# Two mixture stages of a four-block vision network: gate order and Pool adds in the first, up banks and takes in the last

## What is computed

```python
def _L0_ffn_ref(x, gate_w, gate_b, W1, b1, W2, b2):        # 2048 tokens of 64, E = 8 experts of width 128
    probs = softmax(xf @ gate_w + gate_b)
    top2_vals, top2_idx = top_k(probs, 2)
    cw = zeros((N, E)).at[arange(N)[:, None], top2_idx].add(top2_vals)
    for e in range(E):
        acc = acc + cw[:, e, None] * (gelu(xf @ W1[e] + b1[e]) @ W2[e] + b2[e])

def _L3_ffn_ref(h, gate_w, gate_b, w1, b1, w2, b2):        # 8 experts of width 256
    probs = softmax(x @ gate_w + gate_b)
    idx, prb = argmax(probs), max(probs)
    pos = place of the token among those of its expert;  kept = pos < C
    y = (relu(x @ w1[idx] + b1[idx]) @ w2[idx] + b2[idx]) * (prb * kept)
    y = nan_to_num(y, nan=0.0, posinf=1e4, neginf=-1e4)
```

## Time and profile before

| what | value |
|---|---|
| three runs | 539.71, 541.76, 542.22 us (median 541.76) |
| the profiled execution's own time | 541.19 us |
| its span, first to last instruction | 539.4 us |
| mean granted clock of TensorE | 0.973 of full speed |
| PE busy | 478.7 us (89%), 5459 matmul instructions |
| DVE busy | 328.7 us (61%) |
| ACT busy | 293.0 us (54%) |
| POOL busy | 140.1 us (26%) |
| first mixture, from its first up to its last add | 126.94 to 168.71 us of the span |
| last mixture, from its first up to its last add | 464.3 to 535.9 us |

### The profile page before, as it was taken

One profiled execution on the slowest core, in us unless ns is written; L12 is line 12 of the kernel. 1 busy time (PEld: TensorE's weight loads), 2 busy tenths in 40 slices (PEclk: granted clock), 3 DMA queues, 4 the chain that ended last, 5 costly groups with the idle time before them and its releaser, 6 DMA issues. The chain is left out here.

```text
span 539.4 us, 12786 instructions
## 1 busy us (share of the span) xinstructions
PE 478.7 (89%) x5459; PEld 255.5 (47%) x5464; DVE 328.7 (61%) x575; ACT 293.0 (54%) x430; POOL 140.1 (26%) x134
## 2 busy tenths in 40 slices
PE   4799998998996999878998999997997998999992
PEld 1343432554333496778788744343223335533330
DVE  1285999455356366677777746758554593554565
ACT  2583223526651236988788636674683171665561
POOL 8170000000064000599999920003402000000000
PEclk9999999998998899999999998999899889999998
DMA  7000000002661002855565200011003000001000
GB/s 271 2 2 2 1 2 1 1 12 104 162 155 34 2 1 63 293 206 194 202 201 196 81 6 18 0 67 48 0 1 125 0 2 1 2 21 40 1 18 22
DMA packets 9801, 34.52 MB, mean 64 GB/s; under 512 B 1248, under 2 KB 2704, under 8 KB 9360
## 3 DMA queue, kind: packets, MB, share of 16 engines
q1 hardware_dynamic: 9744, 33.70, 19.5%
HBM read 32.94 MB, written 0.75 MB: 62 GB/s over the span
## 5 line engine op out<-in xcount | busy, mean ns | idle before, releaser
L1096 PE MATMUL PS<-GX,OH 128*128 128x64 f16 x1152 | 70.4, 193 | 10.0 <-DVE OH L1279 7.1
L1202 ACT ACTIVATE OHU<-BC,wbuf 128x2048 fp8e4<-128x2048 f16 x36 | 70.0, 1994 | 12.5 <-PE PS L1096 8.8
L1096 PEld LDWEIGHTS PS<-GX,OH 128*128 128x128 f16 x1152 | 67.6, 98 | 15.1 <-DVE OH L1279 8.9
L1096 PE MATMUL PS<-GX,OHU 128*128 128x64 f16 x1152 | 70.1, 193 | 0.1
L1096 PEld LDWEIGHTS PS<-GX,OHU 128*128 128x128 fp8e4 x1152 | 67.6, 98 | 0.1
L1035 POOL TENSOR_TENSOR VAL<-V 128x256 f32<-128x256 f32 x35 | 38.8, 1108 | 2.7
L708 DVE SCALAR_TENSOR_TENSOR D<-QKVP,wbuf,D 128x1024 f32<-128x1024 f32 x27 | 34.6, 1281 | 7.7 <-ACT D L608 6.9
L1032 POOL TENSOR_TENSOR V<-SQ 128x512 f32<-128x512 f32 x18 | 25.1, 1394 | 49.9 <-DVE SQ L1289 48.6
L437 PE MATMUL PS<-T,DG 128*32 128x512 f32 x336 | 37.1, 594 | 0.0
L1996 PE MATMUL PS<-Y,wbuf 64*128 64x512 f32 x128 | 35.6, 618 | 0.1
L2069 ACT ACTIVATE HID<-PS,wbuf 128x512 f32<-128x512 f32 x44 | 28.7, 689 | 10.4 <-PE PS L1996 10.3
(11 more groups left out here) (296 smaller groups left out, 920.3 us busy)
## 6 DMA issues: line engine op xcount, KB each, us to landing
BC<-idx_dram SPq DMA_DIRECT2D x36, 512.0 KB, 4.3
GB<-gate_dram SPq DMA_DIRECT2D x16, 256.0 KB, 7.2
wbuf<-pack_dram SPq DMA_DIRECT2D x1, 1913.0 KB, 9.3
wbuf<-pack_dram SPq DMA_DIRECT2D x1, 1624.0 KB, 6.7
wbuf<-pack_dram SPq DMA_DIRECT2D x1, 1494.0 KB, 6.1
wbuf<-pack_dram SPq DMA_DIRECT2D x1, 871.0 KB, 4.3
wbuf<-pack_dram SPq DMA_DIRECT2D x1, 788.0 KB, 10.8
wbuf<-pack_dram SPq DMA_DIRECT2D x1, 607.0 KB, 3.8
```

The lines of the kernel that those rows point to most:

```text
L1096: mm = pe.matmul(o, (OH, OHU)[qh][:, s % NOH, t * P:(t + 1) * P], src, start=(qh == 0 and part == 0), stop=(qh == 1 and part == 1))
L1202: act.activation(OHU[:, s % NOH, :], BC[:, s % NBC, :], ACT.Abs_reciprocal_sqrt, bias=wt("hitq"), scale=HIT, saturate=False).then_inc(uppe ...
```

## The change

In the first mixture:

- TensorE waits for the logits to be read ahead of its first up. The first seven up matmuls use seven banks (4 to 7, then 0 to 2) without a wait; later ones use banks 4 to 7. Five up steps come first, then the gates' transpose, then down 0; behind that two downs and two ups take turns to the end. Downs 0 to 2 wait until the up in their bank is emptied.
- SP loads the gates of expert 0 in two half rows (18 loads instead of 16).
- ACC is gone. VectorE adds T of expert 0 into X, GpSimd adds T of experts 1 to 6 into X, and VectorE adds T of expert 7 behind GpSimd's sum.

In the last mixture:

- From unit 24 (SIX) on, ups use six banks (6, 7, 4, 5, 2, 3); downs use two banks (0, 1) instead of three.
- In chunks of two j, the evacuation and the take of the second j are done a chunk later (`settled`). Masks have four buffers and are made at the start of a chunk's work on VectorE (`mine`).
- VectorE takes every odd hidden unit from 12 on, six more than before.
- The last j (DIRECT) is not evacuated: VectorE scales the sum so far, then reads the out bank, adds the bias, multiplies by SCB and copies by mask (`take_direct`).

```diff
@@ first mixture: SP, GpSimd, TensorE
-                for e in range(E):
-                    if e >= 4:
-                        sp.wait_ge(gates_in[e % 4], 32)
+                for j, (e, first, last) in enumerate(ROWS):
+                    if j >= 4:
+                        sp.wait_ge(gates_in[j % 4], 32 * (j // 4))
...
-                        pool.tensor_tensor(ACC[:, c], a, T[:, k % TBUF, :], ALU.add).then_inc(summed, 1)
+                        pool.tensor_tensor(X[:, c], X[:, c], T[:, k % TBUF, :], ALU.add).then_inc(summed, 1)
...
-                        if n >= 4:
-                            pe.wait_ge(hid_in, n - 3)
+                        if n >= WIDE:
+                            pe.wait_ge(hid_in, up_after(n))
...
-                    if k == 0:
-                        pe.wait_ge(g_exp, 1)
+                    if k < 3:
+                        pe.wait_ge(hid_in, 5 + k)
...
-                for k in range(4):
+                pe.wait_ge(g_exp, 1)
+                for k in range(5):
                     up(k)
-                down(0)
                 pe.wait_ge(gated, 1)
                 pe.transpose(bank(3, P), EXPS[:, :, :].rearrange("p t e -> p (t e)"), wt("ident")).then_inc(gt_ps, 1)
+                down(0)
                 down(1)
-                up(4)
                 up(5)
+                up(6)
                 down(2)
-                up(6)
+                down(3)
                 up(7)
-                down(3)
-                for first, ups in ((4, (8, 9, 10)), (6, (11, 12, 13)), (8, (14, 15))):
-                    for k in ups:
-                        up(k)
-                    down(first)
-                    down(first + 1)
-                for k in range(10, NK):
+                up(8)
+                for k in range(4, NK):
                     down(k)
+                    if k % 2 and k + 4 < NK:
+                        up(k + 4)
+                        if k + 5 < NK:
+                            up(k + 5)
@@ first mixture: VectorE
+                    if e == 0:
+                        dve.wait_ge(weighed, k + 1)
+                        dve.tensor_tensor(X[:, c], X[:, c], T[:, k % TBUF, :], ALU.add).then_inc(first_in, 1)
+                    if e == E - 1:
+                        dve.wait_ge(weighed, k + 1)
+                        dve.wait_ge(summed, pool_sum(E - 2, bp))
+                        ins = dve.tensor_tensor(X[:, c], X[:, c], T[:, k % TBUF, :], ALU.add)
@@ last mixture
-            UBANK, OBANK = (4, 5, 2, 3), (0, 1, 6)
+            OBANK = (0, 1)
+            def up_bank(n):
+                return bank((4, 5, 2, 3)[n % 4] if n < SIX else (6, 7, 4, 5, 2, 3)[(n - SIX) % 6])
+            DIRECT = NJ - 1
+            SIX = 24
+            def settled(i):
+                late = [j for j in CHUNKS[i - 1][1:] if j < DIRECT] if i else []
+                return late + [j for j in CHUNKS[i] if j == CHUNKS[i][0] or j >= DIRECT]
             def on_dve(n):
-                return n % 2 == 1 and n >= ALONE and (n < 16 or n % 8 != 7)
+                return n % 2 == 1 and n >= ALONE
...
-                        if n >= 4:
+                        if n == SIX:
+                            pe.wait_ge(cum_in, 1)
+                            pe.wait_ge(sc_row, 1)
+                        elif n > SIX:
+                            wait_hidden(pe, n + bh - 6)
+                        elif n >= 4:
                             wait_hidden(pe, n + bh - 4)
...
-                    if n % 4 == 0 and j >= 3:
-                        pe.wait_ge(out_in, j - 2)
+                    if n % 4 == 0 and j >= 2:
+                        pe.wait_ge(out_in, j - 1)
...
+                def take_direct(j):
+                    bp, e = j // E, j % E
+                    dve.wait_ge(hid_used, 4 * j + 4)
+                    after(dve, dve.scalar_tensor_tensor(out=OUT8[:, j % 2, :], in0=bank(OBANK[j % 2]), scalar=wt("b2c", e, 1),
+                                                        in1=SCB[:, bp * HC:(bp + 1) * HC], op0=ALU.add, op1=ALU.mult))
+                    after(dve, dve.copy_predicated(SUM8[:, bp, :], MINE[:, j % 4, :], OUT8[:, j % 2, :]))
...
                 for i, chunk in enumerate(CHUNKS):
+                    if len(chunk) > 1:
+                        for j in settled(i):
+                            mine(j)
                     if i + 1 < len(CHUNKS):
                         for j in CHUNKS[i + 1]:
                             for n in range(4 * j, 4 * j + 4):
                                 if on_dve(n):
                                     hidden(n)
-                    for j in chunk:
+                    for j in settled(i):
+                        if j >= DIRECT:
+                            if j == DIRECT:
+                                scaled(1)
+                            take_direct(j)
+                            continue
                         if j >= E:
                             first_half(j)
```

More of the change, by code:

```diff
@@ L787, in build, with up_after @@
             T = sb("T2", [P, TBUF, HC], F32, sctx)
[L788 to L790 removed]
+            gated, gt_ps, gt_in, gt_out, hid_ps, hid_in, hid_used, weighed, first_in, summed = (
+                sem("s2_" + n) for n in ("gated", "gt_ps", "gt_in", "gt_out", "hid_ps", "hid_in", "hid_used", "weighed", "first_in", "summed"))
             gates_in = [sem(f"s2_gates_in{i}") for i in range(4)]
             NK = 2 * E
[L793 removed]
+            WIDE = 7
+            ROWS = [(0, 0, HC), (0, HC, COLS)] + [(e, 0, COLS) for e in range(1, E)]
+            def up_bank(n):
+                return (4, 5, 6, 7, 0, 1, 2)[n] if n < WIDE else 4 + (n - WIDE) % 4
+            def up_after(n):
+                return n - 6 if n < WIDE + 4 else n - 3
             def pool_sum(e, bp):
[L797 removed]
+                return 2 * (e - 1) + bp + 1
             @block.sync
@@ L892, in _ @@
                         act.wait_ge(hid_used, n - HBUF + 1)
-                    act.activation(HID[:, n % HBUF, :], bank(4 + n % 4), ACT.Gelu, bias=wt("b1_0", n // 4, 1)).then_inc(hid_in, 1)
+                    act.activation(HID[:, n % HBUF, :], bank(up_bank(n)), ACT.Gelu, bias=wt("b1_0", n // 4, 1)).then_inc(hid_in, 1)
                 warm(act, ACT.Sqrt)
@@ L932, in _ @@
                     c = slice(bp * HC, (bp + 1) * HC)
-                    dve.wait_ge(gates_in[e % 4], 32 * (e // 4 + 1))
+                    j = bp if e == 0 else e + 1
+                    dve.wait_ge(gates_in[j % 4], 32 * (j // 4 + 1))
                     dve.wait_ge(hid_used, 2 * k + 2)
                     before = e - TBUF // 2
-                    if before in ON_POOL:
+                    if before >= 1:
                         dve.wait_ge(summed, pool_sum(before, bp))
[L938 to L951, removed]
+                    if before == 0:
+                        dve.wait_ge(first_in, bp + 1)
+                    dve.scalar_tensor_tensor(out=T[:, k % TBUF, :], in0=bank(k % 4), scalar=wt("b2_0", e, 1), in1=GB[:, e, c],
+                                             op0=ALU.add, op1=ALU.mult).then_inc(weighed, 1)
+                    if e == 0:
[5 more added lines that the diff above has]
+                        ins = dve.tensor_tensor(X[:, c], X[:, c], T[:, k % TBUF, :], ALU.add)
+                        if bp == 0:
+                            ins.then_inc(x_half, 1)
         with ExitStack() as sctx, nc.Block() as block:
@@ L2058, in evacuate @@
                     act.wait_ge(hid_used, 4 * j + 4)
-                    if e and takes(j) > 2:
-                        act.wait_ge(taken, takes(j) - 2)
+                    if e and takes(j - 2) > 0:
+                        act.wait_ge(taken, takes(j - 2))
                     o = OUT8[:, j % 2, :] if e else SUM8[:, bp, :]
-                    act.activation(o, bank(OBANK[j % 3]), ACT.Identity, bias=wt("b2c", e, 1)).then_inc(out_in, 1)
+                    act.activation(o, bank(OBANK[j % 2]), ACT.Identity, bias=wt("b2c", e, 1)).then_inc(out_in, 1)
                 def hidden(n):
@@ L2068, in hidden @@
                         act.wait_ge(hid_used, n - HBUF + 1)
-                    act.activation(HID[:, n % HBUF, :], bank(UBANK[n % 4]), ACT.Relu, bias=wt("b1_3", 2 * e + m, 1)).then_inc(hid_in_a, 1)
+                    act.activation(HID[:, n % HBUF, :], up_bank(n), ACT.Relu, bias=wt("b1_3", 2 * e + m, 1)).then_inc(hid_in_a, 1)
                 hidden(0)
@@ L2135, in gate_work, with mine @@
                         gates()
+                def mine(j):
+                    bp, e = j // E, j % E
+                    if e:
+                        dve.wait_ge(id_in, 32)
+                        after(dve, dve.tensor_scalar(MINE[:, j % 4, :], EID[:, bp * HC:(bp + 1) * HC], float(E - e), None, ALU.is_equal))
                 def take(j):
```

41 lines of the change are left out of this document (21 added, 20 removed).

## The result

| | median us | runs |
|---|---|---|
| before | 541.72 | 539.71 to 542.22 |
| changed | 532.98 | 530.50 to 535.03 |

The account below looks back on a forecast made before the run. It took TensorE, slowed by low clock, late gates and a long tail in the first mixture and bank waits in the last, as the bound; 7.05 + 3.4 + 0.15 = 10.6 us off 541.19 gave 530.6, predicted 530.8, range 527.8 to 534.3.

Parts of the forecast that it names:

- the one on the clock: First mixture, TensorE after the transpose: 25.3 us of downs and ups at full clock, last down ending at 158.25.
- That rival: First mixture: the clock falls all the same, as TensorE idles 1.2 us before its first up; 1.7 us, 532.4; chance 0.13.
- my 36.5: First mixture: 36.5 us from the first matmul of the logits to the last add into X.
- my sum: Whole kernel: gains of 7.05 + 3.4 + 0.15 = 10.6 us, giving 530.6 for the profiled execution.
- the tail: End of first mixture: last add into X done at 161.65, or 160.7 by the lower end, against 168.71.
- The halves of the first row: First mixture: gates of the first half stand at 138.8 to 140.15, their weighing done at 139.6 to 140.95.
- The adds of GpSimd: First mixture: 12 adds instead of 8, 2.5 us per expert, covered by TensorE's 3.78.
- The add that I took at 1.64 us: First mixture's end: VectorE's add beside GpSimd's last add, between 0.69 and 1.64 us, taken as 1.64.
- The last stage: Last mixture: 3.4 us from the up groups and 0.15 us from the direct last take.
- six banks: Last mixture: six up banks remove 0.68 us of waiting from each of five up groups, 3.4 us.
- the later evacuation: Last mixture: evacuation one step later clears the next down by 0.2 us; taken as no gain.
- The clean-up: End of last mixture: starts 2.2 us after the last down; the direct last take gains 0.15 us.

Follow-up runs that it names:

- The execution on record: The first profiled execution of the changed kernel, with no further edit; it took 534.96 us, against a median of 532.98 us.
- The idle filled: Changed kernel plus 11 small matmuls on constants between the logits and the wait ahead of the first up; 529.62 us, ratio 0.980.

## Why the prediction was wrong

**The step that failed** is the one on the clock: "The sum holds at the full clock only", and "now it has ups without a gap from 128.15 to 132.6". The ups were without a gap, and the clock was low all the same. I let the dense ups outweigh the 1.2 us of idle that the change puts ahead of them, which I named only in a rival. Six of six traces with this idle have the low clock at the first ups, none of the four of the new order without it has. Filling the idle, with nothing else changed, took it away: there the cause is shown, in one trace. That rival had a chance of 0.13 and a price of 1.7 us. The price was right for 3.4 us at the low level (37.6 to 37.9 against 36.17: 1.4 to 1.7), but 6.8 us cost 2.9 to 3.3. The execution on record had the long one, and its stage came out 2.9 us above my 36.5. That execution took 4.4 us more than my sum for it (534.96 against 530.6): the 2.9, 1.05 ahead of the stage in code that is the same, 0.3 that the last stage fell short, and 0.1 elsewhere.

**The rest of the first mixture held**, at the full clock. The idle filled gives, from the logits: transpose 7.58 (forecast 7.45), first weighing 13.72 (13.65 to 15.0), from the end of the transpose to the last down 25.4 us (25.3), the tail 2.8 (3.4 with the slow add, 2.45 with the fast one). The halves of the first row came in as fast as the lower end had it. The adds of GpSimd took 1.27 to 1.29 us and were covered, as this view of their line shows (shortest, median, longest in ns):

```profile
L831 POOL TENSOR_TENSOR X<-X,T x12: 1267/1276/1290, 148.0 to 162.4; 128x512 f32<-128x512 f32 x12
```

The add that I took at 1.64 us took 1.37. I had read the earlier trace rows as both engines being stretched at once; here GpSimd's adds are not stretched at all, and VectorE's ends 0.54 us after GpSimd's last (162.88 + 1.37 against 161.21 + 2.50), less than its own 0.69. The Trainium skill (SBUF — State Buffer, Who interferes with whom) has whoever comes second wait for all of the first; that would end the add at 164.40, and it ended at 164.25. The trace agrees with that to 0.15 us, and my reading was the worse one. By the same rule the three long adds of before, VectorE's at 160.99 beside GpSimd's third (which ends at 161.35), GpSimd's fourth at 161.31 and VectorE's at 161.93, would end at 162.04, 163.17 and 163.71; they ended at 161.90, 163.02 and 163.57. So they took turns, in either order of the two engines, and were not stretched at once.

**The last stage** gave 3.28 of 3.55 us, right in size and partly for other reasons: six banks 2.3, not 3.4, and the later evacuation 1.6 where I had nothing. These two overlap with the other edits and do not add up to a ledger; what the masks and the six moved units give alone was not tried. That the sum came out within 0.3 us is therefore partly luck: one term was too large and another missing. The margin of the downs behind the later evacuation, 0.2 us in the sum, was as thin as that: in four of the down groups the evacuation released a weight load, after 0.36 us of idle where the two before it have 0.29 and 0.28, and the down groups still took 3.58 us:

```profile
496.28 0.14 PEld L2030 LDWEIGHTS PS<-HID,wbuf 128*64 128x64 f32 x2 [0.36 <-ACT OUT L2084]
```

The clean-up started 2.13 us after the last down, close to the forecast (2.2).

**The base** had low clock of its own in the first mixture, 1.4 us, which I counted as gain. It went only to be replaced by that of the idle.

**What stays open** is the rest of the total. The stretch between the two changed stages took from 288.4 to 296.0 us in traces of identical code, with more time at the low level in the slower ones: 3.7 us in the shortest, 20.5 in the longest. Whether the clock falls there by chance or by what goes before, no run here tells, nor why the low stretch at the first ups lasted 3.4 us in three traces and 6.8 in three. In the traces of the three measurements of the changed kernel the stretch between took 295.4, 290.5 and 294.6 us, which fits their ratios of 0.988, 0.981 and 0.986; it is one trace of each. My range, with 1.7 us of clock in it, was too narrow for it on the upper side. And that the median of all 16 runs, 530.6, lies beside my 530.8 says little: the kernel before had medians from 538.6 to 541.7 beside them.

## What to carry to other kernels

Where an edit makes TensorE wait, price not only the wait but the granted clock of the work behind it, even where that work is dense and the wait itself is covered: 1.2 us of idle, free in itself, cost 1.4 to 3.3 us of clock. It need not happen every time: behind the first four ups of the old order 1.59 us of idle brought the low level in one of two traces. A wait that guards a late step belongs in front of that step, or behind enough work that is ready. And before a gain is forecast from one trace, look for low clock in the very stage: part of the gain may be only its absence.

## What the runs showed of the hardware

- The clock fell within 1.17 us of idle, after 16 small matmuls of the logits (1.86 us), and stayed low into dense ups: 3.4 us in three traces, 6.8 in three, of the same instructions. With 11 small matmuls in place of the idle it stayed at 1.00.
- An add of VectorE beside GpSimd's took 1.37 to 1.39 us in the nine traces of the new tail, and 0.69 without it, while GpSimd's 12 adds stayed between 1.26 and 1.31.
